# Local attention in a decoder block: the first head pair's softmax division on ACT in place of GpSimd

## What is computed

```python
q = l2norm(q) * qs
k = l2norm(k) * ksc
q, k = rotary_xpos(q, k)
...
bk, bv = (look_around(bk), look_around(bv))
sim = jnp.einsum('bhwid,bhwjd->bhwij', bq, bk)
mask = (i < j) | (i > j + WINDOW) | (j == -1)
sim = jnp.where(mask, -jnp.finfo(sim.dtype).max, sim)
attn = jax.nn.softmax(sim, axis=-1)
out = jnp.einsum('bhwij,bhwjd->bhwid', attn, bv)
...
x = x + o @ wo
```

## Time and profile before

| | us |
|---|---|
| median of 3 runs | 2108.06 |
| lowest, highest | 2107.99, 2108.07 |
| span of the profiled execution (first to last instruction) | 2101.9 |
| busy in it: PE, DVE, ACT, POOL | 2009.2, 1663.8, 1481.0, 1351.8 |

### The profile page before, as it was taken

How to read it: one execution, slowest core, us unless ns; L and a number is a source line. 1 busy time by engine, 2 the same in 40 slices (tenths; PEclk the granted TensorE clock), 3 DMA queues, 4 the chain that set the end, 5 groups by cost and what they waited for, 6 DMA issues and landing times.

```text
span 2101.9 us, 47112 instructions
## 1 busy us (share of the span) xinstructions
PE 2009.2 (96%) x15216; PEld 1465.4 (70%) x15216; DVE 1663.8 (79%) x3989; ACT 1481.0 (70%) x3418; POOL 1351.8 (64%) x1378
## 2 busy tenths in 40 slices
PE   5999999999999999789999998999899999999997
PEld 4445555555555554368989887888688898887887
DVE  7888888888888889478888886565488888886775
ACT  2688888888888888557777776554377777775443
POOL 3445566544444443778989885554488888875775
PEclk8899999999999999899999999999999999999999
DMA  4233333433333335256554553100355545551211
GB/s 136 82 110 115 115 106 116 129 120 111 115 115 126 134 136 173 73 120 146 109 129 101 117 111 100 57 16 1 85 110 110 128 104 117 109 117 50 65 59 46
DMA packets 191083, 216.30 MB, mean 103 GB/s; under 512 B 24128, under 2 KB 117056, under 8 KB 190848
## 3 DMA queue, kind: packets, MB, share of 16 engines
q1 hardware_dynamic: 188288, 204.90, 36.1%
q0 software_dynamic: 2560, 8.39, 1.1%
HBM read 47.14 MB, written 29.89 MB: 37 GB/s over the span
## 4 chain that ended last, share of the span: by engine, by line
PE 86%; DVE 6%; POOL 2%; ACT 2%; SPq 2%; issue 2%; DMA 1%; POOLq 0%; ACTq 0%; DVEq 0%
PE PS L685 11%; PE PS L522 11%; PE PS L524 10%; PE PS L523 10%; PE PS L669 10%; PE PS L654 5%; PE PS L775 5%; PE PS L799 5%; PE PS L784 4%; PE PS L590 4%; PE PS L759 2%; PE PS L636 2%; PE PS L702 2%; SPq L1565 2%; DVE MX L1102 1%
## 5 line engine op out<-in xcount | busy, mean ns | idle before, releaser
L1102 DVE TENSOR_REDUCE MX<-PS 128x1 f32<-128x512 f32 x1024 | 641.9, 682 | 96.0 <-PE PS L654 92.7
L927 ACT ACTIVATE PT<-PS 128x512 f32<-128x512 f32 x1024 | 552.3, 614 | 93.0 <-PE PS L669 90.3
L669 PE MATMUL PS<-QS,KS 64*128 64x512 f32 x1024 | 365.8, 436 | 6.7 <-ACT PT L927 4.7
L654 PE MATMUL PS<-KS,QS 64*128 64x512 f32 x1024 | 350.9, 432 | 4.2 <-DMA KS<-HL 0.9
L669 PEld LDWEIGHTS PS<-QS,KS 64*128 64x128 f32 x1024 | 164.3, 185 | 251.9 <-issue 216.3
L1472 POOL TENSOR_TENSOR PB<-PB,RC 128x512 f32<-128x512 f32 (+1 forms) x256 | 273.2, 1077 | 53.9 <-DVE RC L1224 53.9
L685 PE MATMUL PS<-PT,VP 128*17 128x512 f32 x2048 | 270.3, 600 | 4.1 <-ACT OT L934 3.2
L988 ACT ACTIVATE PB<-PB,NMf 128x256 f32<-128x256 f32 (+1 forms) x512 | 245.5, 490 | 12.4 <-DVE NMf L1215 12.1
L1215 DVE CUSTOM_DVE_ANT_0 PB<-PS,mk 128x256 f32<-128x256 f32 (+1 forms) x512 | 178.3, 386 | 62.1 <-PE PS L775 55.8
L1452 POOL TENSOR_TENSOR RI<-RI,mhalf 128x8 f32<-128x8 f32 x128 | 212.8, 1662 | 10.7
L654 PEld LDWEIGHTS PS<-KS,QS 64*128 64x128 f32 x1024 | 168.3, 187 | 48.0 <-issue 36.5
(11 more groups left out here) (188 smaller groups left out, 4797.0 us busy)
## 6 DMA issues: line engine op xcount, KB each, us to landing
qT<-QN SPq DMA_DIRECT2D x384, 128.0 KB
kT<-kT SPq DMA_DIRECT2D x256, 128.0 KB
od<-OT SPq DMA_DIRECT2D x64, 256.0 KB, 2.7
QS<-HL SPq DMA_DIRECT2D x96, 128.0 KB
KS<-HL SPq DMA_DIRECT2D x96, 128.0 KB
QS<-HL SPq DMA_DIRECT2D x48, 256.0 KB
KS<-HL SPq DMA_DIRECT2D x48, 256.0 KB
OC<-od SPq DMA_DIRECT2D x32, 256.0 KB
```

Of the source, the lines that this page charges most:

```text
L654: pe.matmul(PS[:, bank, :], QS[rows, s, h // 2, qt * P:(qt + 1) * P], KS[rows, s, h // 2, :], start=True, stop=True).then_inc(fills("amax" ...
L669: pe.matmul(PS[:, bank, :], KS[rows, s, pair, kt * P:(kt + 1) * P], QS[rows, s, pair, :], start=True, stop=True).then_inc(fills("score", v ...
L927: act.activation(PT[:, kt % 2, 2 * i + half], PS[:, TURNS["score", vb, g, kt, half, i][0], :], ACT.Exp).then_inc(drains("score", vb, g, kt ...
L1102: dve.tensor_reduce(MX[:, vb % 2, h // 8, qt, c:c + 1], PS[:, TURNS["amax", vb, h, qt][0], :], AX, ALU.max).then_inc(drains("amax", vb, h, ...
```

## The change

The entry `wscale` of the first pair (`hp` 0) is done by ACT, the other three pairs' stay on POOL. `WINDOW_ORDER` is as before, so on ACT the new work stands where `("wscale", 0, 0)` stands in the list. On ACT it is two instructions, one for a head, each a copy with the head's column of `RC` as scale; on POOL it was one for both heads. A semaphore of its own, `p_scaled_act`, tells of it. PE's transposes of the first pair wait for that one, and DVE's reciprocals wait for both.

```diff
@@ -19,6 +19,7 @@
 LAG = 11
+SCALED_BY_ACT = (0,)
...
@@ -511,6 +512,11 @@
+        def scaled(L, u, hp):
+            on_act = hp in SCALED_BY_ACT
+            own = [k for k in range(4) if (k in SCALED_BY_ACT) == on_act]
+            return sem["p_scaled_act" if on_act else "p_scaled"], len(own) * (NU * L + u) + own.index(hp) + 1
+
...
@@ -777,7 +783,7 @@
             def wpt(L, u, hp):
                 js = (0, 1) if u % 4 else (1,)
-                pe.wait_ge(sem["p_scaled"], nth("wscale", L, u, hp))
+                pe.wait_ge(*scaled(L, u, hp))
...
@@ -999,6 +1005,15 @@
+            def wscale(L, u, hp):
+                if hp in SCALED_BY_ACT:
+                    k0 = 0 if u % 4 else P
+                    act.wait_ge(sem["recip"], nth("wrecip", L, u, hp // 2))
+                    for hh in (2 * hp, 2 * hp + 1):
+                        p = PB[:, u % 2, hh, k0:]
+                        m = act.activation(p, p, ACT.Copy, scale=RC[:, u % 2, hh:hh + 1])
+                    m.then_inc(sem["p_scaled_act"], 1)
+
...
@@ -1219,7 +1234,8 @@
             def wrecip(L, u, g):
                 dve.wait_ge(sem["expd"], nth("wexp", L, u, 2 * g + 1))
                 if u >= 2:
-                    dve.wait_ge(sem["p_scaled"], nth("wscale", L, u - 2, 2 * g + 1))
+                    for hp in (2 * g, 2 * g + 1):
+                        dve.wait_ge(*scaled(L, u - 2, hp))
...
@@ -1468,8 +1484,9 @@
-                pool.wait_ge(sem["recip"], nth("wrecip", L, u, hp // 2))
-                pool.tensor_tensor(p, p, RC[:, u % 2, h].unsqueeze(2).broadcast_to([P, 2, 256 - k0]), ALU.mult).then_inc(sem["p_scaled"], 1)
+                if hp not in SCALED_BY_ACT:
+                    pool.wait_ge(sem["recip"], nth("wrecip", L, u, hp // 2))
+                    pool.tensor_tensor(p, p, RC[:, u % 2, h].unsqueeze(2).broadcast_to([P, 2, 256 - k0]), ALU.mult).then_inc(sem["p_scaled"], 1)
```

More of the change, by code:

```diff
@@ L383 @@
     [f"qkv_in{k}" for k in range(5)] + [f"mlp_in{k}" for k in range(14)] + ["qkv_hi", "qkv_lo", "mlp_hi", "mlp_lo"] +
-    ["sq", "sumsq", "sumsq_max", "rnorm", "roped", "qk_normed", "qkt_hi", "expd", "wpv", "q_pad", "recip", "p_scaled", "o_hi"] +
+    ["sq", "sumsq", "sumsq_max", "rnorm", "roped", "qk_normed", "qkt_hi", "expd", "wpv", "q_pad", "recip", "p_scaled", "p_scaled_act", "o_hi"] +
     ["xd_zero", "xs_in0", "xs_in1", "mstats", "mmean", "mvar", "mrstd", "hn", "ht_hi", "ht_lo", "gate5", "u_hi", "u_lo", "y_in", "x_res",
@@ L1045, in mup @@
                 m.then_inc(sem["u_hi"], 1)
-            does = dict(split_w=split_w, tr_hi=tr_hi, ctx_hi=ctx_hi, rope_out=rope_out, bias1_out=bias1_out, heads_hi=heads_hi, val_out=val_out,
+            does = dict(wscale=wscale, split_w=split_w, tr_hi=tr_hi, ctx_hi=ctx_hi, rope_out=rope_out, bias1_out=bias1_out, heads_hi=heads_hi, val_out=val_out,
                         negmax=negmax, score=score, ot=ot, out_hi=out_hi, split_qkv=split_qkv, split_mlp=split_mlp, wtrh=wtrh, wsq=wsq, wv=wv, wqkh=wqkh,
```

## The result

| | before | after |
|---|---|---|
| median, us | 2108.02 (4 runs, 2107.40 to 2108.07) | 2120.07 (4 runs, 2118.66 to 2121.77) |
| span of the profiled execution | 2101.9 | 2117.2 |
| busy PE, DVE, ACT, POOL | 2009.2, 1663.8, 1481.0, 1351.8 | 2015.8, 1692.2, 1525.7, 1293.5 |

The ratio of the runs is 1.0062, 95% interval 1.0049 to 1.0075: 0.6% slower, 12 us by the medians and 10 to 16 by the interval. The forecast was 2123.6 us by the median and 2117.4 by the span.

A forecast was written before the change was run, and what follows sets the result against it. PE was taken as the bound, busy 249.61 of 250 us in the steady stretch. Stops of 13.2 us plus 2.3 at the stage ends, 15.5, put on the median of 2108.06 gave 2123.6 us, range 2114 to 2130.

The forecast's parts named there:

- The moved work: ACT's two scalings per step, priced like the exponential of the same tile: 0.80 us in a wide step, bounds 0.60 and 0.98.
- Kind 1: Every fourth step, number 1 modulo 4: PE's output projection stops 0.85 us without a weight-splitting piece on ACT, 1.13 with one.
- What is absorbed: Part of the stops falls on PE's existing wait for half-swapped keys, 0.4 at most: 13.2 of 13.6 us remain.
- the sum: Both attention stages together: 13.2 us of stops plus 2.3 at the stage ends, 15.5 us slower.
- Kinds 0, 2 and 3: The other pipeline steps, by number modulo 4: OTr is late, but PE's slack of 0.99 or 1.84 us covers it; nothing.
- The stage ends: Last steps of both attention stages: late OTr delays PE by 0.8 us in the first layer, 1.5 in the second.
- that gain is put at nothing: First stage's last steps: PE's shorter wait for the first scaling saves nothing, as ACT's comes hardly sooner than POOL's.
- A: Rival, no change: PE takes in the late OTr and XT, only the ends remain, 2108 to 2110.5 us; chance 0.12.
- B: Rival, knock-on: after late DVE, each of 14 steps costs 0.3 to 0.6 us more, 2127 to 2131 us; chance 0.18.
- its first half: Late DVE's next sum of two tiles meets POOL's third-pair scaling, which starts first; the sum takes 1.0 us longer.
- Its second half: Normalized keys and last pair's scaling, ready only 0.2 us before PE's use, come late: 4 to 8 us in all.
- C: Rival, faster: at the stage ends POOL's first scaling comes back whole in four steps, 4.6 us, 2103.4 us; chance 0.04.

The follow-up runs named there:

- the second pair: The kernel before and the changed kernel, both as they are, for a second profiled execution each: 2120.76 us against 2105.62, ratio 1.0065.

## Why the prediction was right, and where

**The moved work.** The scaling's pitch was taken as 0.40, with bounds 0.30 and 0.49 for one: measured 0.41 (two in 0.82), each 502 ns long. The idea to take the exponential for a model held.

**Kind 1.** Forecast 0.85 without a piece and 1.13 with one; measured 0.83 and 1.11, and 1.03 in the two steps whose piece is smaller, which I had counted with the others. 8 x 0.83 + 4 x 1.11 + 2 x 1.03 = 13.1, against 13.6. Each step of the chain came as written. The hidden 0.15 between DVE's XT and PE's first matmul (0.05 and 0.1, both estimates) was exactly the measured 0.15.

**What is absorbed.** Forecast 0.4. The twelve stops between window 1's projection and window 28's, with the 0.18 of step 29, make 11.9 over both stages. The first pair of traces shows 9.7 there, the second pair 11.5: about 2 absorbed in one and 0.4 in the other. The step behind a stop is 0.05 to 0.10 shorter. The rest goes by waits that one execution has and another hasn't, for the half-swapped keys as the prediction had it: in step 14 of the first trace of before PE idles 0.39 for them, and the same step of the change is 0.66 shorter; the second trace of the change has such a wait of 1.12, in step 4. What the sum lacked in both pairs is in step 2 of the first stage, where PE's wait for DVE's X falls from 1.39 to 0.70: window 0's projection to window 1's was 14.35 us and is 13.41, which gives back the first stop. With the scalings behind XT, where there is no stop, it is 13.36, so the late PE is not the reason; the reason stays open.

**Kinds 0, 2 and 3.** Nothing, as forecast: their steps keep their length, though ACT waits for the reciprocals in kinds 0, 2 and 3 too (0.36, 0.41 and 0.24 us; the prediction had near nothing for kinds 2 and 3). The run with kind 1 on POOL showed it by itself.

**The stage ends.** Forecast 0.8 + 1.5 = 2.3; PE's wait for OTr and for ACT's scalings moved windows 28 to 30 by 0.6 and 1.1 (0.5 and 0.7 in the second pair), and the last step by about what the clock lost. "The wait for OTr takes over: that gain is put at nothing" held: of POOL's 2.9 there remain 0.5, plus 2.1 for ACT. But the pair of spans had 5.0 us on the last steps, of the clock, that no term of the sum named. The sum met the span because it had 4 too much in its own terms (15.5 for 11.6), 5 too little for the clock, and 1.3 came off before the first attention stage.

**From the span to the median.** The prediction put the whole sum on the median as on the span, and read the 6.2 us between the two as a constant ("which I leave as it is"). That reading was wrong. In every run since then the time is 1.7 to 1.9 above that run's own span; the other 4.4 of the 6.2 was that the profiled execution of before was a quick one. The clock didn't fall at its ends, and in the second trace, where it did, the last steps are 4.2 longer. Adding the sum to the median was right nonetheless, since the falls are in the typical run of both kernels (17 of 24 ends). The sum's own stretches measured 11.6 us in the first pair of traces and 12.9 in the second, against the 15.5 of the sum: the waits that vary, the first stage's step 2 and the ends each took a part. The medians give 12.1 and 15.1 and their intervals 10 to 16 and 9 to 18, so the times alone don't tell 12 from 15.5; the traces do, within the us or two by which they differ from one another. The mechanism was right, and that the result lies near the forecast isn't luck; that the first two spans agree to 0.2 is.

One more slip, which the result did not touch: the prediction puts the forecast's low end at 2116, but its own bounds (14 x 0.2 less, nothing at the ends) give 2108.1 + 13.2 - 2.8 = 2118.5.

**The rivals.** *A*, no change: fell, PE had next to no slack (0.05). *B*: its first half came true. More of DVE's sums now find a scaling under way on POOL: 944 ns in the mean for 687, 33 us more on DVE, while POOL's scaling keeps its mean (1163 for 1156 ns). The Trainium skill, "SBUF — State Buffer", section "SBUF: two separate sides", has GpSimd and a DVE instruction with two SBUF inputs take a port pair exclusively, whichever starts first keeping the other out. In the trace of the change that holds: 44 of the 128 sums take 1.43 to 1.44, in each of them the scaling had started first, and where the sum starts first it keeps its 0.66 to 0.70 and POOL's scaling is the long one, mostly 1.40 to 1.46 for a wide one in place of 1.04. Step 21 has both:

```profile
1174.02 1.46 POOL L1489 TENSOR_TENSOR PB<-PB,RC 128x512 f32<-128x512 f32 x1 [0.64 <-DVE RC L1240]
1179.38 1.04 POOL L1489 TENSOR_TENSOR PB<-PB,RC 128x512 f32<-128x512 f32 x1
1179.54 1.43 DVE L1210 TENSOR_TENSOR RA<-RA,RB 128x512 f32<-128x512 f32 x1
```

The 1.71 of the earlier trace rows doesn't fit: there the sum's row starts 0.09 before POOL's, and yet it is the sum that is long, as in three other traces at that place; why stays open. So the prediction's reading of it, that it is mostly POOL that loses, held for before only. The lateness of DVE isn't the whole reason either: with the scalings behind XT, where DVE isn't late, 42 sums are long. Its second half didn't come: in the two runs with the scalings behind XT, which have the long sums as well, PE is busy 250.00 and 249.94 of 250. *C*, faster by POOL's relief: not at the old place, and not at a better one either (0.9998 and 0.9994, both intervals with 1 in them).

**What stays open.** What decides in one execution whether the clock falls at a stage's end: in all twelve traces PE idles 2.2 to 2.5 us for TT just before, and at 17 of 24 ends the clock fell then, at 7 it didn't. With kind 1 on POOL it fell once behind shorter waits. No run here took the wait for TT away. Open too is why the first stage's step 2 is 0.9 shorter with the change.

## What to carry to other kernels

An engine with a quarter of its time free is not free at every place: where a wait and some work are put in front of a hand-over, add the lateness of both and hold the sum against the consumer's slack in the tightest kind of step (here 0.9 and 0.8 us were each nearly covered, their sum of 1.7 stopped the bound engine 14 times, and the same work a few entries later on the list cost nothing). Work taken from an engine that isn't the bound bought nothing here, even where its new place was free (ratios 0.9998 and 0.9994). Before a trace's span is set against a median, take time less span of one and the same run, and look for stretches in which the granted clock differs.

## What the runs showed of the hardware

The granted clock fell to 0.50 at 17 of 24 stage ends, right behind 2.2 to 2.5 us of idle PE, at both ends in one trace of before and at neither in the other, and a fall went with a last step longer by 1.4 to 3.2 us. Over the runs of before on two chips the span goes with the mean clock: at 0.983 it is 2103.8 and 2102.6 in the mean (8 and 3 runs), at 0.979 it is 2108.0 and 2107.8 (5 and 4 runs). So a good part of the scatter between runs of this kernel, some 10 us, goes with the clock, and a single pair of traces can't be read to better than about 5 us at its ends (an estimate, from the 4.2 us by which the last steps of the two traces of before differ).

A copy with a column as scale of 128x256 on ACT takes 502 ns and the next instruction can start 0.41 after it, as with the exponential. Its 128 wide form took 395 ns.
